# Thirteen large tiles of a fused attention and MoE-FFN kernel begin 128 or 384 bytes lower in SBUF

## The reference, cut to what matters

```
x = x + tanh(g_xattn) * xattn(layernorm(x), ctx, pos)     # q, k, v; rope on q and k; softmax; attn @ Wout + bout
x = x + tanh(g_ffn)  * ffn(layernorm(x))

def ffn(h):
    logits = h @ gate_w                                   # 512 x 8
    routing_weights, _ = top_k(logits, 2)
    shared = square(relu(h @ up_w)) @ down_w              # 512 x 2048, 2048 x 512
    moe = (h @ expert_weight) * routing_weights.sum(-1)   # 512 x 512
    y = shared + moe
    return (y - mean(y)) * rsqrt(var(y) + eps) * gamma + beta
```

## Time and profile before

| | |
|---|---|
| median of 3 runs | 1622.49 us (1620.65 to 1623.03) |
| the profiled execution | 1620.87 us |
| its span, first to last instruction | 1619.1 us |
| PE busy | 1562.0 us, 96% |
| DVE, ACT, POOL busy | 975.4, 638.3, 295.5 us |
| granted TensorE clock over the span | 0.991 |
| attention alone | to about 774 us |
| FFN, block 0 begins | 773.6 us |
| blocks 1 to 7 begin | 884.8, 989.0, 1092.5, 1196.9, 1300.1, 1404.5, 1507.8 us |

### The profile page before, as it was taken

One profiled execution on the slowest core, in us unless ns is written; L12 is line 12 of the kernel. 1 busy time (PEld: TensorE's weight loads), 2 busy tenths in 40 slices (PEclk: granted clock), 3 DMA queues, 4 the chain that ended last, 5 costly groups with the idle time before them and its releaser, 6 DMA issues.

```text
span 1619.1 us, 26178 instructions
## 1 busy us (share of the span) xinstructions
PE 1562.0 (96%) x9883; PEld 1166.3 (72%) x9883; DVE 975.4 (60%) x1448; ACT 638.3 (39%) x962; POOL 295.5 (18%) x370
## 2 busy tenths in 40 slices
PE   8699999999999999988999999999999999999997
PEld 6456666666666666655787887887878878788786
DVE  7587788788777778865662634436445354353524
ACT  4165555555555555566442222222222222222221
POOL 5222222222222222201000201002011020010202
PEclk9799999999999999999999999999999999999999
DMA  6624444554443444343540100101101011010101
GB/s 176 135 64 107 110 117 108 126 126 120 119 103 102 106 109 122 84 113 94 155 125 1 53 27 32 32 17 47 32 20 40 20 47 33 8 52 20 52 1 39
DMA packets 67191, 121.22 MB, mean 75 GB/s; under 512 B 12280, under 2 KB 25720, under 8 KB 67064
## 3 DMA queue, kind: packets, MB, share of 16 engines
q1 hardware_dynamic: 67064, 119.50, 27.6%
HBM read 51.17 MB, written 16.78 MB: 42 GB/s over the span
## 4 chain that ended last, share of the span: by engine, by line
PE 83%; DVE 10%; issue 2%; ACT 1%; POOL 1%; DMA 1%; SPq 1%; POOLq 0%; DVEq 0%; ACTq 0%
PE pP L984 16%; PE pA L1180 11%; PE pO L984 11%; PE pB L1180 11%; PE pT L984 9%; PE pA L1075 6%; PE pO L1103 6%; PE pM L984 4%; DVE mneg L1399 4%; PE pB L1091 2%; PE pT L991 2%; PE pM L991 2%; PE pP L991 2%; PE pM L1147 1%; DVE rot L1327 1%
## 5 line engine op out<-in xcount | busy, mean ns | idle before, releaser
L1399 DVE TENSOR_REDUCE mneg<-pA 128x4 f32<-128x1024 f32 x250 | 305.7, 1223 | 139.4 <-PE pA L1075 137.5
L887 ACT ACTIVATE probs<-pB 128x1024 f32<-128x1024 f32 x249 | 255.2, 1025 | 267.1 <-PE pB L1091 246.3
L1502 DVE TENSOR_TENSOR relu<-relu 128x512 f32<-128x512 f32 x128 | 88.3, 689 | 257.3 <-ACT hid L937 257.3
L704 POOL TENSOR_SCALAR var_eps<-meanvar 128x1 f32<-128x1 f32 x96 | 34.6, 360 | 1058.1 <-DVE meanvar L1284 1057.9
L1180 PE MATMUL pA<-dn,hid 128*128 128x512 f32 x768 | 198.8, 394 | 0.9 <-DVE hid L1504 0.2
L1180 PE MATMUL pB<-dn,hid 128*128 128x512 f32 x768 | 196.0, 390 | 0.0
L984 PE MATMUL pP<-fT,up 128*128 128x512 f32 x768 | 190.3, 396 | 0.0
L984 PE MATMUL pO<-fT,up 128*128 128x512 f32 x768 | 187.5, 393 | 0.0
L1180 PEld LDWEIGHTS pA<-dn,hid 128*128 128x128 f32 x768 | 143.1, 188 | 36.2 <-DVE hid L1504 4.8
L984 PEld LDWEIGHTS pO<-fT,up 128*128 128x128 f32 x768 | 144.4, 188 | 32.3 <-issue 0.4
L1180 PEld LDWEIGHTS pB<-dn,hid 128*128 128x128 f32 x768 | 144.2, 188 | 31.0
(11 more groups left out here) (201 smaller groups left out, 1991.5 us busy)
## 6 DMA issues: line engine op xcount, KB each, us to landing
stk<-kT SPq DMA_DIRECT2D x180, 128.0 KB, 2.9
stq<-qT SPq DMA_DIRECT2D x180, 128.0 KB, 3.0
fres<-x_scratch SPq DMA_DIRECT2D x34, 256.0 KB, 2.8
xin<-x SPq DMA_DIRECT2D x32, 256.0 KB, 2.9
xres<-x SPq DMA_DIRECT2D x32, 256.0 KB, 3.5
x_scratch<-xres SPq DMA_DIRECT2D x32, 256.0 KB, 2.4
out<-y_s SPq DMA_DIRECT2D x32, 256.0 KB, 2.0
fx<-x_scratch SPq DMA_DIRECT2D x29, 256.0 KB, 2.7
```

What stands on the lines that cost most here:

```text
L704: nc.gpsimd.tensor_scalar_add(var_eps[:], meanvar[:, 1:2], EPS).then_inc(ve_made, 1)
L887: nc.scalar.activation(probs[:, s % 4, :, :, :].rearrange("p a b s -> p a (b s)"), psum[:, :, :], ACT.Exp).then_inc(exp_done, 1)
L1399: nc.vector.tensor_reduce(mneg[par][:, :, 2 * u:2 * u + 2].rearrange("p t q -> p q t"), psum[:, :, :].rearrange("p q (t k) -> p q t k", t= ...
L1502: nc.vector.tensor_tensor(r[:], r[:], r[:], ALU.mult).then_inc(sq_made, 1)
```

## The change

Two edits in the two lists of tiles; no instruction, wait, order, shape or size changes, and the instructions of all five engines stand in the same order as before.

```
@@ attention's tiles
         attn = [sb1(f"attn{t}", [P, D]) for t in range(TT)]
-        rden = [sb1(f"rden{i}", [P, NH // 2]) for i in range(2)]
         aT = [sb1(f"aT{i}", [P, KC, P], F32R) for i in range(2)]
         xres = [sb1(f"xres{i}", [P, D]) for i in range(2)]
         gbout = sb1("gbout", [P, D])
+        rden = [sb1(f"rden{i}", [P, NH // 2]) for i in range(2)]
         mneg = [sb1(f"mneg{i}", [P, TT, NH]) for i in range(2)]
@@ the FFN's tiles
         fT[0] = [sb2(f"fT0{j}", [P, KC, BLK], F32R) for j in range(2)]
-        gt_s = sb2("gt", [P, KC, 2 * NEXP], F32R)
-        gt_raw = sb2("gt_raw", [P, KC, NEXP])
         fx = sb2("fx", [P, D])
@@
         route = [sb2(f"route{i}", [P, UT]) for i in range(2)]
+        gt_s = sb2("gt", [P, KC, 2 * NEXP], F32R)
+        gt_raw = sb2("gt_raw", [P, KC, NEXP])
         second.close()
```

## The result

The changed kernel took 1611.8 us (median of 6 runs, 1609.65 to 1613.4) against 1621.47 for the kernel before in the same series (6 runs). The ratio is 0.9938, 95% interval 0.9926 to 0.9951: 9.7 us less, where 9.5 were forecast. The time forecast was 1613.0 us; of the 1.2 us by which it missed, 1.0 is that the kernel before has a lower median over six runs (1621.47) than over the first three (1622.49). The profiled span went from 1619.1 to 1609.4 us. Measured once more on another occasion, the ratio was 0.9952 (0.9936 to 0.9969), 7.9 us between the medians.

A forecast was written before the change was run, and what follows sets the result against it. PE's pace of starting matmuls was taken to bound the FFN. Gains of 6.7, 1.0, 1.2 and 1.0 us make 9.9, less 0.4 is 9.5; 1622.49 less 9.5 gives 1613.0 us, range 1611.0 to 1617.5.

The forecast's parts named there:

- PE's rate follows the pair of starts: FFN and attention matmuls: start every 227 ns where moving and stationary operand begin at one rest, otherwise every 232.5.
- Odd blocks, 1.68 us each, 6.7 in all: FFN rounds of blocks 1, 3, 5, 7: 14 rounds 0.11 us less, two 0.07 less; 6.7 us in all.
- Even blocks, 1.0 + 1.2 us: Blocks 0, 2, 4, 6: rounds gain 1.0 us at the hidden-shared switch, experts u = 1 to 3 gain 1.2 us.
- Attention, 1.0 us: wo with aT: O1 0.04 us less, both halves of O0 0.03 together, 15 iterations; bounds 0 and 2.0 us.
- The first expert gains nothing: Even blocks: first expert 0.08 us quicker, but the shared matmuls' wait for DVE's hid grows by 0.08.
- `gt`, the transposes, DVE, ACT and POOL stay: Tiles that move without gain: routing's matmuls 0.35 us at most, transposes 0.9 at most, both taken as 0; busy times stay.
- The sum: Whole kernel: terms of 9.9 us, less 0.4 for rounds behind fx transposes, give 9.5 us less.
- A: FFN blocks: parity stands for something other than the address, so nothing changes, 1622.5 us; chance 0.06.
- B: FFN: odd blocks only become what even ones are now, attention gains nothing; 6.4 us less, 1616.1 us; chance 0.15.
- C: FFN: crowding at one rest puts every matmul at 232.5 ns, 14 us slower, 1636.5 us; chance 0.03.

The follow-up runs named there:

- mirror image: The changed kernel with 384 bytes of gap before fT[0] and 1664 before fT[1], so odd and even blocks swap addresses; 1619.51 us, ratio 0.9985.

## Why the prediction was right, point by point

- **PE's rate follows the pair of starts.** Right, and shown from both sides: the mirror image turned odd and even round, and three kernels with other distances became slower than the kernel before. The argument in the prediction rested on two distances only. It was not only the pair, though: the prediction called `shared` quick in both parities, but its own rows 4 give 2.76 us for it in odd blocks, slowed by the `hidden` in front. The sum didn't suffer, since it was made of whole rounds. That the rule is about 256 bytes, and that 64 costs less than 32, wasn't in it; modulo 2048 was enough for this change, but was more than is needed.
- **Odd blocks, 1.68 us each, 6.7 in all.** The rounds of block 7, which have no transposes of `fx`, went from 85.75 to 84.07 us, 1.68 less to the digit. Blocks 1, 3 and 5 gained 1.44 to 1.48. Sum 6.1. The term was too large by 0.6, and for the reason that the prediction gave with too small a sum (0.4): behind four transposes PE needs up to ten matmuls to get back to 227 ns, however the tiles lie.
- **Even blocks, 1.0 + 1.2 us.** Blocks 2, 4 and 6 gained 0.30, 0.49 and 0.48 where 0.28 + 0.31 was worked out for each. Their rounds gained 0.18 each, since the eight with or behind the transposes gained 0.05 together and not 0.16; the experts gained 0.3 each in blocks 4 and 6, as forecast. In block 2 of the first profile one last start of the block came 0.29 us late, which the second profile doesn't have. Block 0's experts gained 0.27 (16.99 to 16.72), but the block as a whole nothing (+0.2 in one profile, -0.1 in the other): its first `shared` waited 0.16 us before, and 0.9 and 0.6 after, by the profile for DVE's `hid`. This is the term most over-sized, by 0.9 us, about half of it block 0's.
- **Attention, 1.0 us.** By the traces right: 0.07 us an iteration forecast, 0.05 to 0.10 measured. Its two parts were split wrongly: `O1` gained 0.03 (to the end of the last matmul it takes 3.04 us, not 3.02), and the halves of `O0` together 0.04. By the runs it was too small: about 2 us or a little more, where the prediction had put its upper bound.
- **The first expert gains nothing.** Right; the wait grew by 0.06 us (0.08 forecast).
- **`gt`, the transposes, DVE, ACT and POOL stay.** Right: transposes as above, DVE 975.4 and 975.7 us busy, ACT 638.3 and 638.7, POOL 295.5 and 296.5.
- **The sum.** 6.1 + 1.3 + 1.1 = 8.5 us by the traces (7.0 and 7.8 us of the FFN in two profiles, 0.8 to 1.5 of attention) against 9.5. The first median shows 9.7, the second 7.9; 8.5 lies within both intervals. By the runs the FFN's edit gave 7.5 us where the prediction had 8.5 (with the 0.4 taken off), and attention's some 2 where it had 1.0. The two errors are of one size and opposite, and that the sum came so close is luck.
- **Rivals.** A fell with the mirror image. The port rule of the Trainium skill ("SBUF — State Buffer", "Who interferes with whom": two independent read ports, TensorE waits for no one) does not hold as a forecast of PE's rate: 2.72 and 2.80 us for the same twelve matmuls of `expert` stand against it. B (odd blocks only as good as even ones of before, 6.4 us) fell too: rounds settle at 5.44, not 5.46. C fell: with everything at one rest, 896 or 0, `shared` runs at 2.72 us per twelve.

## What to carry to other kernels

Where PE runs matmuls back to back and each one loads new weights, let the moving and the stationary operand's tiles begin at addresses that agree modulo 256 bytes; the easy way is to put small tiles last, or to round them up to 256. It is worth up to 6 of 233 ns a matmul, 2.6%, and only where PE sets the pace. Products that take turns should share the rest too: each switch between rests that differ by 128 modulo 256 cost 10 ns here (5.46 against 5.44 us a round). To find such a loss, compare two stretches of a trace that run the same instructions on different tiles, and read starts, not durations.

## What the runs showed of the hardware that I had not expected

- Starts of 512-column matmuls with new weights each, by the distance of their tiles modulo 256: every 226.7 ns at 0, about 229 at 64, 232 to 233.5 at 32, 96, 128, 192 and 224. A gap of 32 bytes costs as much as one of 128.
- A distance of 64 ran at 229 ns in even blocks and at 233.4 in odd ones of one kernel, behind different neighbours. So there is a state that outlasts the group; what it is stays open.
- One unequal tile in three slows two intervals in three (233, 234, 227 ns).
- A slow product can slow an equal one behind it for seven matmuls (231 to 236 ns with one of 224 between; kernel before, odd blocks).
- Why the distance matters at all, banks of the memory or the meeting of two reads, no run here shows.
